# Global attention: TensorE's work ordered by whole steps in place of half steps

## The reference

```
q, k = rope(proj(Wq)), rope(proj(Wk));  v = proj(Wv)
scores  = einsum('bhqd,bhkd->bhqk', q, k) / sqrt(16)      # causal mask
weights = softmax(scores)
out     = einsum('bhqk,bhkd->bhqd', weights, v)
```

## Time and profile before

| | us |
|---|---|
| median of three runs | 3445.2 (3440.74 to 3447.95) |
| the profiled execution | 3442.12, its span 3440.4 |
| global attention's steps, within that span | 158.1 to 1667.8 |
| PE busy in the whole span | 3080.8 (90%) |
| DVE busy | 2413.1 (70%) |
| ACT busy | 1714.0 (50%) |

### The profile page before, as it was taken

One profiled execution on the slowest core, in us unless ns is written; L12 is line 12 of the kernel. 1 busy time (PEld: TensorE's weight loads), 2 busy tenths in 40 slices (PEclk: granted clock), 3 DMA queues, 4 the chain that ended last, 5 costly groups with the idle time before them and its releaser, 6 DMA issues. The chain is left out here.

```text
span 3440.4 us, 77045 instructions
## 1 busy us (share of the span) xinstructions
PE 3080.8 (90%) x31756; PEld 1909.2 (55%) x31756; DVE 2413.1 (70%) x4236; ACT 1714.0 (50%) x3173; POOL 953.9 (28%) x1011
## 2 busy tenths in 40 slices
PE   7799999999999999999868998968987999986996
PEld 6333333334443333434457777757876777765875
DVE  7699999987889997875246666645555666664555
ACT  5267777887778888887223333322223333332222
POOL 8410000000110000001035545532224555542223
PEclk9699999999999999999789999989998999998998
DMA  8420001000020000000220000000000000003001
GB/s 255 127 63 17 9 9 46 9 9 18 25 69 17 9 9 10 5 8 8 73 91 20 20 14 20 32 28 6 0 5 31 20 16 19 20 26 112 0 0 49
DMA packets 61014, 113.91 MB, mean 33 GB/s; under 512 B 9240, under 2 KB 25368, under 8 KB 60056
## 3 DMA queue, kind: packets, MB, share of 16 engines
q1 hardware_dynamic: 56600, 103.07, 9.6%
q10 hardware_dynamic: 4096, 6.30, 0.7%
HBM read 75.00 MB, written 33.55 MB: 32 GB/s over the span
## 5 line engine op out<-in xcount | busy, mean ns | idle before, releaser
L650 DVE TENSOR_REDUCE mp<-ps_m 128x2 f32<-128x1024 f32 (+3 forms) x1152 | 1275.8, 1134 | 192.5 <-PE ps_m L701 134.8
L628 ACT ACTIVATE probs<-ps_s 128x512 f32<-128x512 f32 (+3 forms) x2304 | 1162.1, 561 | 380.5 <-PE ps_s L725 349.7
L741 PE MATMUL ps_o<-probs,vall 128*32 128x256 f32 (+3 forms) x9216 | 711.1, 380 | 15.4 <-POOL probs L605 9.1
L725 PE MATMUL ps_s<-qst,kst 64*128 64x512 f32 (+3 forms) x2304 | 595.7, 486 | 4.3 <-ACT probs L628 2.9
L701 PE MATMUL ps_m<-kst,qst 64*128 64x512 f32 (+3 forms) x2304 | 481.3, 401 | 33.1 <-DVE mp L650 15.7
L725 PEld LDWEIGHTS ps_s<-qst,kst 64*128 64x128 f32 x2304 | 241.3, 187 | 459.3 <-ACT probs L628 398.9
L741 PEld LDWEIGHTS ps_o<-probs,vall 128*32 128x32 f32 x9216 | 186.0, 109 | 342.1 <-issue 177.0
L701 PEld LDWEIGHTS ps_m<-kst,qst 64*128 64x128 f32 x2304 | 233.3, 192 | 77.1 <-DVE mp L650 57.8
L594 POOL TENSOR_TENSOR msplit<-negm,mzero 128x16 fp32r<-128x16 f32 x32 | 7.2, 224 | 907.0 <-DVE negm L656 907.0
L1020 POOL TENSOR_TENSOR a_rot<-a_scr 128x512 f32<-128x512 f32 x128 | 163.4, 1277 | 321.3 <-DVE a_scr L1376 321.3
L605 POOL TENSOR_SCALAR_AFFINE_SELECT probs<-probs 128x256 f32<-128x256 f32 x256 | 103.0, 406 | 513.0 <-ACT probs L628 512.9
(11 more groups left out here) (189 smaller groups left out, 5411.7 us busy)
## 6 DMA issues: line engine op xcount, KB each, us to landing
a_tab<-in_rope SPq DMA_DIRECT2D x32, 512.0 KB
q_parts<-pparts SPq DMA_DIRECT2D x32, 256.0 KB, 3.6
k_parts<-pparts SPq DMA_DIRECT2D x32, 256.0 KB, 3.9
qst<-q_parts SPq DMA_DIRECT2D x64, 128.0 KB, 2.7
o_raw<-o_sb SPq DMA_DIRECT2D x32, 256.0 KB, 2.0
X<-in_x SPq DMA_DIRECT2D x8, 512.0 KB, 5.7
kst<-k_parts SPq DMA_DIRECT2D x32, 128.0 KB, 3.7
qst<-q_parts SPq DMA_DIRECT2D x64, 64.0 KB, 2.6
```

The lines of the kernel that those rows point to most:

```text
L628: act.activation(probs[:, s % PR, h, off:C], sslots[n % SR][:, off:C], ACT.Exp, scale=float(D) ** -0.5).then_inc(exp_done, 1)
L650: dve.tensor_reduce(mp[b % 2][:, h:h + 2, cc:cc + 1], slot[:, :, 0:width], AX.X, ALU.max).then_inc(max_read, 1)
L725: pe.matmul(sslots[n % SR][:, off:C], kst[g % 2][rows, hp, i * P:(i + 1) * P], qst[q_slot(b)][rows, hp, off:C], start=True, stop=True).the ...
L741: last = pe.matmul(ps_o[32 * h:32 * h + VW, lo:hi], vall[:, i, (g * GH + h) * DV:(g * GH + h) * DV + VW], probs[:, s % PR, h, lo:hi], star ...
```

## The change

The loop goes over steps. In step s TensorE does both weighting halves of step s-1, the scores of heads 0 and 1 of step s+1, the units of both half steps, and the scores of heads 2 and 3 of step s+1. No instruction is added, removed or altered, on any engine; the waits inside `score`, `weigh` and `do` are what they were. `plan` and the order of the units among themselves stay too.

```
-            for t, (_, todo) in enumerate(plan):
-                s, hp = t // 2, t % 2
+            for s in range(NSTEP):
                 if s >= 1:
-                    weigh(s - 1, hp)
+                    weigh(s - 1, 0)
+                    weigh(s - 1, 1)
                 if s + 1 < NSTEP:
-                    score(s + 1, hp)
-                for unit in todo:
+                    score(s + 1, 0)
+                for unit in plan[2 * s][1] + plan[2 * s + 1][1]:
                     do(unit)
+                if s + 1 < NSTEP:
+                    score(s + 1, 1)
```

## The result

The changed kernel takes 3558.6 us (median of four runs, 3551.6 to 3565.7), against 3443.0 (3440.7 to 3447.9): a ratio of 1.034 with a 95% interval of 1.033 to 1.036. The forecast was 3530, between 3478 and 3592; the measured time lies at the upper edge of the 3500 to 3560 that the forecast itself named. The profiled execution took 3551.6 with a span of 3549.8, 109 more than the one of before. The first weighting starts at 162.47 and the last at 1774.17, so the attention's steps take 1611.7 in place of 1509.7: 102 of the 109 lie there. 4.4 lie before it and 3 behind it, in code that wasn't touched.

What follows compares the result with a forecast made beforehand. Prediction: TensorE's order (1.23 a half step) and the third-score-slot loop (1.24) both bind; the new loop is 2.66 a step. Terms +37, +29, +9 and +10 sum to +85, profiled 3442.1 to 3527, forecast 3530; range 3478 to 3592.

Steps and rivals of the forecast that it cites:

- The loop of 2.66: Ordinary step: head 0's scores to head 3's 1.24, to weighting 0.43, both halves 1.00; together 2.67, 2.66 used.
- The path through the third slot: Score slots: head 3's score waits for head 0's exponent of the same step, 0.59 + 0.60 + 0.05 = 1.24 us.
- The second weighting half at 0.43: TensorE's weighting: the second half behind the first takes 0.43 us, 1.00 for both; bounds 0.43 and 0.57.
- the same, among key loads: Sixteen full two-unit steps held by ScalarE's issues of key loads, exponents 3.68 apart; longer than the new loop, so unchanged.
- full, three units: 61 full steps whose third max unit waits for the first's reduction: 3.62 from mean 3.15, +29 us; bounds 0.15 and 0.58.
- The diagonal: 28 blocks, five steps around each diagonal, VectorE's reductions next to bind: 11.47 to 11.83, +10 us; bounds -5 and +20.
- The array's saving: Rival: head 3's wait isn't binding, so TensorE's saved time shortens ordinary steps; about -67 us, 3378; chance 8%.
- its deciding point: For the array's saving to come through, the loop must be under 2.54, so the 1.24 must be 1.12 or less.
- The wash: Rival: slack on TensorE removes disturbances, three-unit steps cost only 0.15, the diagonal gains 5; +31 us, 3476; chance 12%.
- The unsaved half: Rival: the second weighting half saves nothing, loop 2.80, 403 full steps cost 0.14 more; +56 us, 3586; chance 8%.
- The clock rival: Rival: waiting in each step brings more stretches at the lower clock in the attention, 15 more; +75 us, 3605; chance 7%.
- The signs to look for: Profile signs, among them 2.66 a step, 16 weighting matmuls in 1.00, L725 loads' idle up, ScalarE's idle up some 80.

Runs made afterwards that it cites:

- the first experiment: Against the changed kernel, the max units go back to their own halves while both weighting halves stay together: 3633.0 us, ratio 1.057 to the kernel before.
- the fourth: Against the changed kernel, ScalarE's wait for the weighting moves from before head 0's exponent to before head 1's of the step before: 3529.1 us, ratio 1.028.
- the slots: Four kernels with at most one max unit a step: order of before with three score slots 3376.7 us, four 3292.3; changed order with three 3525.9, four 3255.5.
- The array's saving comes through only where the slot is given (the fourth-slot run): Changed order with at most one max unit a step, one max slot and four score slots: 3255.5 us; order of before with four slots 3292.3.
- the three regroupings tried here: Changed kernel 3558.6 us; the same with max units back in their halves 3633.0; the same with the weighting halves apart 3637.1.

## Why the prediction was right

**The loop of 2.66.** Right, to the hundredth. Of the 305 ordinary steps 292 lie under 2.72, their median is 2.668 (2.478 before). The path through the third slot was read from the kernel before. Of these only the earlier trace rows show the wait. In the earlier trace rows the pair's loads aren't spread, their 0.41 of idle time is what a pair behind a weighting half shows in the earlier trace rows too, put down to "issue" there, and 1.24 of loop can't be told from 1.23 of TensorE's work. What proves the path is that the first experiment, the fourth and the slots each move the step by what it should give.

**The second weighting half at 0.43.** Right: 1.00 for both. That two halves behind each other cost only their passes at full clock as well was a guess from the earlier trace rows, where the clock was half and the columns were 128; the guess came true.

**The sum.** Step lengths of the two profiled executions, in the prediction's classes:

| class | steps | forecast | measured |
|---|---|---|---|
| full, two units | 305 | +37 | 775.2 to 820.5: +45 |
| the same, among key loads | 16 | 0 | +1 |
| full, three units | 61 | +29 | 192.3 to 227.8: +35 |
| full, none or one | 37 | +9 | 89.0 to 101.2: +12 |
| with a diagonal, and the rest | 155 | +10 | +8 |
| the attention in all | | +85 | +102 |
| outside it | | 0 | +7 |

Two terms were mis-sized. The ordinary steps average 2.69 and not 2.66: 13 of them are disturbed (among the first steps of a block, and in stretches at the lower clock) and hold 7 us over the median. I had taken a mean on the one side of the subtraction, 2.54 with its disturbances, and an undisturbed loop on the other. The three-unit steps have 3.73, the value that the working gave, where I then took 3.62 for narrow first units: only 7 of the 61 have one (2.96 to 3.61), and disturbances make up for them, which is luck for the 3.73. The 7 us outside the attention aren't the changed order's: the order of before with ScalarE's earlier wait spends 3430.6 - 1492.9 = 1937.7 there, the changed kernel 1938.1, and the profiled execution of before 1930.7. Why that one is shorter, and the further 7 between the profiled execution and the median of the changed kernel, have no cause that I can show.

**The diagonal.** Its total came out near the forecast, but not step by step: the medians of the five steps are 2.45, 2.23, 2.33, 2.43 and 2.71, where 2.44, three times 2.27 and 2.58 were forecast. That the total fits so well is partly luck. VectorE's pace is there to see in these rows of the changed kernel: eight reductions in 8.79 us without a gap, from the block's second diagonal step on. The 2.71 has ScalarE's copy of the sums at its end, for which the next weighting waits.

```profile
1305.22 8.79 DVE L650 TENSOR_REDUCE mp<-ps_m 128x2 f32<-128x1024 f32 x8 [0.69 <-PE ps_m L701]
...
1313.27 0.16 PEld L741 LDWEIGHTS ps_o<-probs,vall 128*32 128x32 f32 x8 [0.80 <-ACT o_sb L615]
```

**The rivals.** The array's saving comes through only where the slot is given (the fourth-slot run), so its deciding point was placed rightly. The wash gave an ordinary step 0.06 more and a three-unit step 0.15; they took 0.15 and 0.58 more. The unsaved half is refuted by the 1.00. The clock rival too: the mean granted clock is 0.958, against 0.954, and in the attention 0.98 against 0.97. The Trainium skill's rule that a change of tiling mode drains TensorE (TensorEngine Tiling (Array Packing), Key Properties) agrees with the 1.00 for two halves against 1.14 apart; taken alone it gives the wrong sign.

**The signs to look for.** Two of them were wrong. I expected the idle time of L725's loads on L628 to rise; it fell, from 398.9 to 352.7. In the kernel before, as in the earlier trace rows, the idle time noted at these loads is for the most part the 0.41 in which they stand behind the weighting's matmuls; that it is put down to the exponent doesn't make it the exponent's. One such 0.41 in each step went with the change. And ScalarE's idle time on L725 rose by 164, twice the forecast of 80. All its idle time before exponents rose by 135, and that is about the 102 of a longer stage and 31 of busy time that its exponents need less (1162.1 to 1130.7), because more of them now run one behind the other and overlap; the other 29 were put down to other releasers before.

## What to carry to other kernels

Before an engine's work is regrouped to save set-up, write down the ring that each buffer makes: who refills it, who frees it, and what now stands between the two in each in-order queue. With three slots for four heads every step has waits that need some 1.2 us on both sides of it, and half steps filled both sides with other work; in the three regroupings tried here, work moved to one side left the other waiting. A saving on an engine counts only as far as the next loop allows, here it took one more slot.

## What was not expected of the hardware

The page's busy time of TensorE hid all of this: in the stretch of the attention it is 1477.9 before and 1476.8 after, with two changes of array mode fewer in each step, an added wait of 0.4, and 102 us more of span. Durations in these rows overlap and include waiting behind others; only distances between starts told the two orders apart.

A second wait before an instruction had a price that the traces show: ScalarE's exponent with two waits started 0.59 after its scores, with one 0.53, and in a loop each of these 0.06 counted in full. The trace of the changed kernel shows what stands there. Each of the 572 exponents with two waits (head 0, from the fifth step on) has a semaphore instruction of its own in front of it, at L627:

```profile
L627 ACTq EVENT_SEMAPHORE  x572: 17/17/17, 170.2 to 1772.0; - x191
```

It starts 0.06 before the exponent (median). With the wait moved to head 1 it runs while head 0's exponent is at work, and head 1's exponent still starts 0.49 after it.
